# A recommendation model's embedding sums on TensorE: two units counted in a row, then their eight sums

## The chip, the cores and the metric

The kernel runs on one core of one Trainium2 chip. The metric is the device time of one execution in microseconds (us), the median of several runs. Each core has five engines with queues of their own: TensorE (PE), ScalarE (ACT), VectorE (DVE), GpSimd (POOL) and SyncE (SP, which here only starts transfers). They wait for each other by semaphores.

## What is computed

The reference is a recommendation model: a small network on 13 dense features, sums of 20 looked-up rows in each of 26 tables, all pair products of the 27 vectors of a sample, and a second network. What matters here is the sum of looked-up rows.

```
x = _mlp(dense_x, bot, sigmoid_last=False)
pooled = jax.vmap(lambda tab, ix: jnp.take(tab, ix, axis=0).sum(axis=1))(tables, indices)
Tcat = jnp.concatenate([x[:, None, :], jnp.transpose(pooled, (1, 0, 2))], axis=1)
Z = jnp.einsum('bim,bjm->bij', Tcat, Tcat)
R = jnp.concatenate([x, Z[:, li, lj]], axis=1)
return _mlp(R, top, sigmoid_last=True)
```

There are 2048 samples, 26 tables of 12500 rows by 64 numbers, and 20 indices per sample and table.

## The kernel before

Five of the 26 tables are gathered by POOL with indirect transfers (L598) and summed on DVE (L1071). The other 21 (TP in the code) are never gathered. For them the kernel builds, for each block of 512 samples, a matrix of counts (how often does sample b use row r), and multiplies the table with it on PE. A table has four blocks.

**Counting.** A block's samples lie in 86 groups of 6. Four groups make a unit, so a block has 22 units (UNITS), the last with two groups only. DVE builds one-hot factors for a pair of units at a time (`onehot_pair`, L1037 and L1042), in two buffers. PE multiplies them (`count_unit`, L659): eight matmuls of 60 rows by 99 columns for a unit, four for the last. A unit's result fills two PSUM banks: banks 0 and 1 for even units, 2 and 3 for odd ones (`unit_ps[u % 2]`). ACT copies it to SBUF as integers (`unpack_unit`, L820), whose bytes are read as fp8 counts afterwards. PE may write unit n only when the copy of unit n-2 is done (the wait at L652), and, for an even unit, when its pair of one-hots is there (L650).

**Summing.** With a block's counts complete, 98 matmuls (`sum_rows`, L678), each of 128 table rows by 512 samples, add up into one bank (`acc[k % 2]`). The table is stored as a high and a low fp16 part; ACT makes them in seven chunks, the high part at L782 and the low at L789, with a subtraction on DVE between (L998). ACT (`take_lo`, L811) and DVE (`pool_bags`, L1048) take the sum away.

**The order.** `phase(t, k, tn, kn)` is written out by hand for PE: it sums block k of table t and counts the next block between, so phase 0 counts block 1, and phase 3 counts block 0 of the next table. Each of its 22 rounds counts one unit and does PER_UNIT = 4 sums; the last 10 sums follow the last round. `await_rows` holds the waits for the counts of the whole block (L671), for a free accumulator (L672) and for the chunks of the table (L674, in phase 0 only). In phase 0, `turn_bags` (L641) stands ahead of unit 6, and behind the phase the transposes of the next table's indices (L633). A table is one turn of a loop; the last table stands behind the loop, and its phase 3 has only sums.

ACT's order is fixed too, unit by unit, with other work between the copies. In phase 3 the high part of a chunk comes after units 5, 8, 12, 15 and 19, the low part after 9, 12, 16 and 19. In phase 0 there is a high part after units 0 and 2, L811 after unit 1, low parts after 4, 6 and 8, a copy of gathered sums (L803) after 10 and the conversion of indices (L795, L797) after 12. In phases 1 and 2 only L811 stands between, after unit 1. DVE works two pairs ahead of PE; before the third pair of phase 0 it has `pool_bags` and the copy of coefficients (L1005). In phase 1 it also takes the maximum of the next table (L970).

Ahead of all this stands the first network (L624), and behind it the pair products (L745) and the second network, which the change doesn't touch.

Of the kernel before, what the change touches and what calls it, by code (L numbers as in the profile page):

```python
# [47 lines left out]
def build(nc, dense_x, indices, tables, w_bot, b_bot, w_top, b_top, out):  # L48
# [6 lines left out]
    SPAN = -(-ROWS // P)  # L55
# [16 lines left out]
    UNITS = -(-GROUPS // UG)  # L72
# [30 lines left out]
    def units_of(u):  # L103
        return range(u * UG, min((u + 1) * UG, GROUPS))

    ctx = ExitStack()
    with ctx:
# [264 lines left out]
        PER_UNIT = 4  # L372
# [244 lines left out]
        def _(pe):  # L617
# [19 lines left out]
            def turn_bags(n, done):  # L637

                pe.wait_ge(piece_free, PIECES + PIECES * done)
                for q in range(GPAIRS):  # L640
                    last = nc.tensor.transpose(bags_ps[:, q * P:(q + 1) * P],  # L641
                                               bags_out[:, 2 * q:2 * q + 2, :].rearrange("p c d -> p (c d)"),
                                               ident[:, :])
                last.then_inc(bags_turned, 1)

            def count_unit(t, k, u, first=False):

                n = UNITS * (BLOCKS * t + k) + u
                if u % 2 == 0:
                    pe.wait_ge(onehots_ready, PAIRS * (BLOCKS * t + k) + u // 2 + 1)  # L650
                if not (first and u < 2):
                    pe.wait_ge(counts_ready, n - 1)  # L652
                r = (PAIRS * k + u // 2) % 2
                for g in units_of(u):
                    x = g % UG
                    sub, lane = u % 2 * SUBS + x // LG, x % LG
                    for h in range(HALVES):
                        rows_h = slice(h * HP, h * HP + HK)
                        last = nc.tensor.matmul(unit_ps[u % 2][:, h, x * HC:(x + 1) * HC],  # L659
                                                onehot_p[rows_h, r, sub, :, lane],  # L660
                                                onehot_c[rows_h, r, sub, :, :, lane].rearrange("p c s -> p (c s)"),
                                                start=True, stop=True)
                        if g == units_of(u)[-1]:
                            last.then_inc(unit_counted, 1)

            def await_rows(t, k, j0, j1):

                n = BLOCKS * t + k
                if j0 == 0:
                    pe.wait_ge(counts_ready, UNITS * n + UNITS)  # L670
                    pe.wait_ge(acc_free, n + 1)  # L671
                for j in range(j0, j1):  # L672
                    if k == 0 and j % CJ == 0:
                        pe.wait_ge(parts_ready, CHUNKS * t + j // CJ + 1)  # L674

            def sum_rows(t, k, j):

                mm = nc.tensor.matmul(acc[k % 2][:, 0:NB], parts[:, j, :],  # L678
                                      count_bytes[k % 2][:, j % COLS, 0:NB, j // COLS],
                                      start=(j == 0), stop=(j == SPAN - 1))  # L680
                if j == SPAN - 1:
                    mm.then_inc(block_summed, 1)
                elif k == BLOCKS - 1 and j % CJ == CJ - 1:
                    mm.then_inc(chunk_used, 1)

            def phase(t, k, tn, kn, bags=False):

                for u in range(UNITS):
                    if bags and u == 6:
                        turn_bags(t, GB * t)  # L690
                    j1 = SPAN if u == UNITS - 1 else PER_UNIT * (u + 1)
                    await_rows(t, k, PER_UNIT * u, j1)
                    count_unit(tn, kn, u)
                    for j in range(PER_UNIT * u, PER_UNIT * (u + 1)):
                        sum_rows(t, k, j)
                for j in range(PER_UNIT * UNITS, SPAN):
                    sum_rows(t, k, j)
# [12 lines left out]
            with pe.Fori(0, TP - 1) as t:  # L710
                phase(t, 0, t, 1, bags=True)
                turn_indices(t + 1)
                phase(t, 1, t, 2)
                phase(t, 2, t, 3)
                phase(t, 3, t + 1, 0)
# [498 lines left out]
```

## Time and profile before

| | |
|---|---|
| median of 3 runs | 3051.23 us (3049.17 to 3052.97) |
| the profiled execution | 3058.61 us, of which span 3056.8 us |
| mean granted TensorE clock | 0.963 of full speed |
| PE busy | 2934.3 us (96%), 24204 matmuls |
| ACT busy | 2182.6 us (71%) |
| DVE busy | 1991.5 us (65%) |
| POOL busy | 1759.3 us (58%) |
| chain that ended last | PE 85%, ACT 7%, issue 5% |

The span runs from the first instruction to the last in one profiled execution. Busy time is time with an instruction at work; matmuls follow each other before the one ahead has ended, so 96% doesn't say that PE is at its peak. The chain is followed back from the last instruction through whatever released each step.

### The profile page before, as it was taken

The page shows a single profiled execution, that of the slowest core. Times are in us where ns is not written, and L with a number is a line of the kernel's source. Part 1 is how long each engine was busy: PE and PEld are TensorE (multiplying, and loading weights), DVE is VectorE, ACT ScalarE, POOL GpSimd, SP SyncE. Part 2 cuts the span into 40 slices and gives each one's busy share as a digit, 9 for nine tenths or more (in the row PEclk, how much of TensorE's full clock was granted, in tenths as well). Part 3 has the DMA queues.
Part 4 walks back from the last instruction along what each step waited for, and adds up shares of the span by engine and source line. Part 5 has one row for each costly group of instructions (what it writes and reads, how often), then busy time and mean ns, then how long its engine had stood idle before and what let it go on. Part 6 is the DMA issues. An engine that isn't in the chain of part 4 may idle for free.

```text
span 3056.8 us, 65500 instructions
## 1 busy us (share of the span) xinstructions
PE 2934.3 (96%) x24204; PEld 1249.3 (41%) x24204; DVE 1991.5 (65%) x3358; ACT 2182.6 (71%) x2496; POOL 1759.3 (58%) x1640
## 2 busy tenths in 40 slices
PE   6999999999999999999999999999999999999798
PEld 2333343333433333333333333333333333337574
DVE  4477676776767767677676776767767677643221
ACT  3678778777777777877778778777777877872232
POOL 3266676666766667676676666766667676300000
PEclk8899999999999999999999999999999999997668
DMA  2112122121221212212122121221212212007711
GB/s 66 59 29 72 28 72 70 29 72 27 73 69 29 71 28 73 69 30 71 28 73 69 30 71 27 73 69 29 71 28 73 69 30 69 17 25 119 129 35 29
DMA packets 173103, 167.99 MB, mean 55 GB/s; under 512 B 116105, under 2 KB 134329, under 8 KB 167477
## 3 DMA queue, kind: packets, MB, share of 16 engines
q1 hardware_dynamic: 121380, 110.94, 13.2%
q0 software_dynamic: 51200, 52.53, 8.7%
q8 instruction: 238, 3.90, 0.5%
q10 hardware_dynamic: 272, 0.52, 0.1%
q14 instruction: 13, 0.10, 0.0%
HBM read 143.83 MB, written 20.05 MB: 54 GB/s over the span
## 4 chain that ended last, share of the span: by engine, by line
PE 85%; ACT 7%; issue 5%; SPq 1%; DMA 1%; DVE 0%; ACTq 0%; POOL 0%; DVEq 0%; POOLq 0%
PE ps L678 59%; PE ps L659 16%; PE ps L624 5%; PE ps L745 4%; ACT counts L820 4%; ACT parts L782 2%; ACT parts L789 1%; SPq L496 0%; ACT h_bot L833 0%; ACT pooled_sb L811 0%; SPq L519 0%; DMA look_in<-in_r_indices 0%; DMA pooled<-pooled_sb 0%; DMA products<-zt 0%; SPq L503 0%
## 5 line engine op out<-in xcount | busy, mean ns | idle before, releaser
L598 POOL DMA_INDIRECT rows<-in_L_rec_tables,look x1600 | 1745.2, 1091 | 834.3 <-issue 474.2
L820 ACT CAST counts<-ps 128x792 int32<-128x792 f32 (+1 forms) x1848 | 1773.0, 979 | 583.3 <-PE ps L659 571.1
L678 PE MATMUL ps<-counts,parts 128*128 128x512 fp8e3 x8232 | 2178.4, 390 | 0.0
L1037 DVE TENSOR_TENSOR onehot_p<-iota_by_unit,place 128x1024 bf16<-128x1024 bf16 x924 | 636.6, 689 | 639.1 <-PE ps L659 613.4
L678 PEld LDWEIGHTS ps<-counts,parts 128*128 128x128 f16 x8232 | 646.8, 96 | 755.6 <-issue 6.2
L659 PEld LDWEIGHTS ps<-onehot_c,onehot_p 60*128 60x128 bf16 x14448 | 382.4, 95 | 876.1 <-issue 758.2
L659 PE MATMUL ps<-onehot_c,onehot_p 60*128 60x99 bf16 x14448 | 666.5, 209 | 55.0 <-ACT counts L820 35.2
L1042 DVE TENSOR_TENSOR onehot_c<-column_c,weighted_s 128x792 bf16<-128x792 bf16 x924 | 521.7, 565 | 0.0
L1071 DVE TENSOR_REDUCE rows<-rows 128x64 f32<-128x384 f32 (+1 forms) x240 | 188.1, 784 | 9.0 <-DVE pooled_sb L1048 9.0
L998 DVE SCALAR_TENSOR_TENSOR raw<-raw,coef_next,parts 128x896 f32<-128x896 f32 x147 | 168.4, 1146 | 18.1 <-ACT parts L782 18.1
L381 DVE COPY zt<-ps 32x208 f32<-32x208 f32 x128 | 64.8, 507 | 152.4 <-PE ps L745 150.5
L1048 DVE SCALAR_TENSOR_TENSOR pooled_sb<-ps,coef,pooled_sb 64x512 f32<-64x512 f32 x84 | 62.0, 738 | 145.8 <-ACT pooled_sb L811 145.8
L782 ACT ACTIVATE parts<-raw,coef_next 128x896 f16<-128x896 f32 x147 | 155.8, 1060 | 1.0
L970 DVE TENSOR_REDUCE rowmax<-raw 128x1 f32<-128x896 f32 x147 | 156.1, 1075 | 0.0
L1024 DVE TENSOR_TENSOR column_c<-iota_by_unit,place 128x2904 bf16<-128x2904 bf16 x84 | 140.5, 1672 | 3.9
L745 PE MATMUL ps<-slots 64*128 64x104 f32 x1024 | 138.9, 456 | 4.2 <-DMA slots<-pooled 4.2
L789 ACT ACTIVATE parts<-raw 128x896 f16<-128x896 f32 x147 | 142.0, 966 | 0.0
L745 PEld LDWEIGHTS ps<-slots 64*128 64x128 f32 x1024 | 138.2, 367 | 6.1 <-issue 6.1
L381 ACT COPY zt<-ps 32x208 f32<-32x208 f32 x128 | 63.4, 496 | 87.6 <-PE ps L745 86.1
L624 PE MATMUL ps<-feats,w_top0T 128*128 128x512 f32 (+1 forms) x128 | 68.5, 677 | 20.1 <-DMA feats<-products 15.4
L811 ACT ACTIVATE pooled_sb<-ps,coef 64x512 f32<-64x512 f32 x84 | 57.4, 683 | 26.1 <-PE ps L678 24.1
L613 POOL MEMSET slots<- 128x1280 f32 x2 | 2.3, 1165 | 120.8 <-PE ps L678 120.8
(82 smaller groups left out, 525.4 us busy)
## 6 DMA issues: line engine op xcount, KB each, us to landing
raw<-in_L_rec_tables SPq DMA_DIRECT2D x21, 1792.0 KB, 8.3
raw<-in_L_rec_tables SPq DMA_DIRECT2D x21, 1344.0 KB, 11.8
rows<-in_L_rec_tables,look POOLq DMA_INDIRECT x1600, 2.5
pooled<-pooled_sb SPq DMA_DIRECT2D x84, 128.0 KB, 2.3
slots<-pooled SPq DMA_DIRECT2D x30, 352.0 KB, 7.9
products<-zt SPq DMA_DIRECT2D x16, 351.0 KB
idx_raw<-in_r_indices SPq DMA_DIRECT2D x42, 79.7 KB
gathered<-bags_t SPq DMA_DIRECT2D x42, 64.0 KB
```

The lines of the kernel that those rows point to most:

```text
L598: nc.gpsimd.indirect_dma_start(rows[:, s, l, :], None, rows_flat, bass.IndirectOffsetOnAxis(ap=look[:, c, s * PL + l:s * PL + l + 1].bitca ...
L624: last = nc.tensor.matmul(into[i % len(into)][0:mm, :], w, x, start=(k == 0), stop=(k == len(terms) - 1))
L659: last = nc.tensor.matmul(unit_ps[u % 2][:, h, x * HC:(x + 1) * HC], onehot_p[rows_h, r, sub, :, lane], onehot_c[rows_h, r, sub, :, :, lan ...
L678: mm = nc.tensor.matmul(acc[k % 2][:, 0:NB], parts[:, j, :], count_bytes[k % 2][:, j % COLS, 0:NB, j // COLS], start=(j == 0), stop=(j == ...
L745: last = nc.tensor.matmul(banks[2 * ((b + half) % 4) + x // 4][:, x % 4 * P:x % 4 * P + GW], tiles[half][:, g, :, :].rearrange("p k s -> p ...
L782: nc.scalar.activation(parts[:, c, 0:D], raw[:, c, :], ACT.Copy, scale=coef_next[:, 2:3]).then_inc(hi_ready, 1)
L789: nc.scalar.activation(parts[:, c, D:2 * D], raw[:, c, :], ACT.Copy, scale=2.0 ** LO_SHIFT).then_inc(parts_ready, 1)
L820: nc.scalar.copy(counts[k % 2][:, :, u * UG * GS:(u * UG + g) * GS].rearrange("p c (g h s) -> p h g c s", h=HALVES, s=HS), unit_ps[u % 2][ ...
L998: nc.vector.scalar_tensor_tensor(raw[:, c, :], raw[:, c, :], coef_next[:, 2:3], parts[:, c, 0:D], ALU.mult, ALU.subtract).then_inc(diff_re ...
L1037: tt(onehot_p[:, r, :, :, :], iota, at, ALU.is_equal)
L1042: tt(onehot_c[:, r, :, :, :, :], cols, mask, ALU.mult).then_inc(onehots_ready, 1)
L1071: nc.vector.tensor_reduce(dst, src, AX.X, ALU.add).then_inc(piece_free, 1)
```

## The change

PE's phase now goes by pairs of units. It waits for the table rows of both, counts the even unit (banks 0 and 1) and the odd unit (banks 2 and 3), and then does the eight sums of both. The last pair is followed by the ten sums left over, so it has 18. Only PE's order changes; the other engines' instructions stay as they are.

```diff
             def phase(t, k, tn, kn, bags=False):
 
-                for u in range(UNITS):
+                for u in range(0, UNITS, 2):
                     if bags and u == 6:
                         turn_bags(t, GB * t)
-                    j1 = SPAN if u == UNITS - 1 else PER_UNIT * (u + 1)
+                    j1 = SPAN if u == UNITS - 2 else PER_UNIT * (u + 2)
                     await_rows(t, k, PER_UNIT * u, j1)
                     count_unit(tn, kn, u)
-                    for j in range(PER_UNIT * u, PER_UNIT * (u + 1)):
+                    count_unit(tn, kn, u + 1)
+                    for j in range(PER_UNIT * u, PER_UNIT * (u + 2)):
                         sum_rows(t, k, j)
                 for j in range(PER_UNIT * UNITS, SPAN):
                     sum_rows(t, k, j)
```

On PE, in the loop's phase 0, units 4 and 5 before (x is the number of matmuls; REGISTER_ALU rows compute the value that the next wait asks for):

```order
L650 REGISTER_ALU
L652 REGISTER_ALU
L659 MATMUL ps<-onehot_c,onehot_p 128x99 x8
L678 MATMUL ps<-counts,parts 128x512 x4
L652 REGISTER_ALU
L659 MATMUL ps<-onehot_c,onehot_p 128x99 x8
L678 MATMUL ps<-counts,parts 128x512 x4
```

and the same two units in the change:

```order
L650 REGISTER_ALU
L652 REGISTER_ALU
L659 MATMUL ps<-onehot_c,onehot_p 128x99 x8
L652 REGISTER_ALU
L659 MATMUL ps<-onehot_c,onehot_p 128x99 x8
L678 MATMUL ps<-counts,parts 128x512 x8
```

The four sums of the even unit moved behind the odd unit's counts, and the odd unit's wait now stands between two runs of counts.

On PE, the end of phase 0 before, from unit 20:

```order
L650 REGISTER_ALU
L652 REGISTER_ALU
L659 MATMUL ps<-onehot_c,onehot_p 128x99 x8
L678 MATMUL ps<-counts,parts 128x512 x4
L674 REGISTER_ALU
L652 REGISTER_ALU
L659 MATMUL ps<-onehot_c,onehot_p 128x99 x4
L678 MATMUL ps<-counts,parts 128x512 x14
L629 ISA
```

and in the change, into the start of phase 1:

```order
L674 REGISTER_ALU
L650 REGISTER_ALU
L652 REGISTER_ALU
L659 MATMUL ps<-onehot_c,onehot_p 128x99 x8
L652 REGISTER_ALU
L659 MATMUL ps<-onehot_c,onehot_p 128x99 x4
L678 MATMUL ps<-counts,parts 128x512 x18
L629 ISA
L633 MATMUL ps<-ident,idx_raw 128x86 x4
L670 REGISTER_ALU
L671 REGISTER_ALU
L650 ISA
L652 ISA
L659 MATMUL ps<-onehot_c,onehot_p 128x99 x16
L678 MATMUL ps<-counts,parts 128x512 x8
```

The last pair has 12 counts and 18 sums in a row. In a phase's first pair the wait for the whole last block covers the second unit too, so its 16 counts stand without a step between.

## Rows read from the trace of the kernel before

**Rows 1.** The page: busy times, and the chain that ended last by engine and line.
```profile
PE 2934.3 (96%) x24204; PEld 1249.3 (41%) x24204; DVE 1991.5 (65%) x3358; ACT 2182.6 (71%) x2496; POOL 1759.3 (58%) x1640
...
PE 85%; ACT 7%; issue 5%; SPq 1%; DMA 1%; DVE 0%; ACTq 0%; POOL 0%; DVEq 0%; POOLq 0%
PE ps L678 59%; PE ps L659 16%; PE ps L624 5%; PE ps L745 4%; ACT counts L820 4%; ACT parts L782 2%; ACT parts L789 1%; SPq L496 0%; ACT h_bot L833 0%; ACT pooled_sb L811 0%; SPq L519 0%; DMA look_in<-in_r_indices 0%; DMA pooled<-pooled_sb 0%; DMA products<-zt 0%; SPq L503 0%
```

**Rows 2.** Windows of a table: length, PE, PEld, DVE, ACT, POOL busy, clock, DMA.
```profile
1419.42:1450.56 31.14, 31.14 (x276) 12.63 (x276) 26.51 (x45) 22.05 (x23) 20.76 (x20) 1.00 0.15 30
1450.56:1481.41 30.85, 30.85 (x271) 12.22 (x272) 20.73 (x41) 21.99 (x23) 23.32 (x24) 1.00 0.14 29
1481.41:1546.25 64.84, 62.22 (x543) 24.68 (x544) 44.45 (x70) 55.00 (x64) 42.79 (x39) 1.00 0.26 77
```

**Rows 3.** Page, groups: line engine op, shapes xcount | busy us, mean ns | idle before.
```profile
L820 ACT CAST counts<-ps 128x792 int32<-128x792 f32 (+1 forms) x1848 | 1773.0, 979 | 583.3 <-PE ps L659 571.1
```

**Rows 4.** Order of time, PE: start us, us, engine line, [idle before]; starts of phases 1 and 2.
```profile
1545.98 0.27 PE L659 MATMUL ps<-onehot_c,onehot_p 60*128 60x99 bf16 x4
1546.18 3.33 PE L678 MATMUL ps<-counts,parts 128*128 128x512 fp8e3 x14
...
1549.74 0.36 PE L659 MATMUL ps<-onehot_c,onehot_p 60*128 60x99 bf16 x8
1550.04 1.08 PE L678 MATMUL ps<-counts,parts 128*128 128x512 fp8e3 x4
1551.05 0.37 PE L659 MATMUL ps<-onehot_c,onehot_p 60*128 60x99 bf16 x8
...
1580.58 0.37 PE L659 MATMUL ps<-onehot_c,onehot_p 60*128 60x99 bf16 x8
```

**Rows 5.** Order of time, ACT, start of phase 2 (unit 0, and L811 after unit 1).
```profile
1581.01 0.98 ACT L820 CAST counts<-ps 128x792 int32<-128x792 f32 x1 [2.99 <-PE ps L659]
...
1583.33 0.68 ACT L811 ACTIVATE pooled_sb<-ps,coef 64x512 f32<-64x512 f32 x1
```

**Rows 6.** Order of time, ACT, in phase 3.
```profile
1496.32 1.04 ACT L782 ACTIVATE parts<-raw,coef_next 128x896 f16<-128x896 f32 x1
1497.26 0.98 ACT L820 CAST counts<-ps 128x792 int32<-128x792 f32 x1
1498.13 0.94 ACT L789 ACTIVATE parts<-raw 128x896 f16<-128x896 f32 x1
1498.98 2.73 ACT L820 CAST counts<-ps 128x792 int32<-128x792 f32 x3
...
1503.34 2.81 ACT L820 CAST counts<-ps 128x792 int32<-128x792 f32 x3
```

**Rows 7.** Order of time, PE: counts behind a wait, in phase 3 and phase 0.
```profile
1504.43 0.36 PE L659 MATMUL ps<-onehot_c,onehot_p 60*128 60x99 bf16 x8 [0.22 <-ACT counts L820]
...
1516.64 0.36 PE L659 MATMUL ps<-onehot_c,onehot_p 60*128 60x99 bf16 x8 [0.79 <-issue]
...
1523.59 0.37 PE L659 MATMUL ps<-onehot_c,onehot_p 60*128 60x99 bf16 x8 [1.61 <-ACT counts L820]
```

**Rows 8.** Waits: engine line waited for, us in total, times, longest us.
```profile
POOL rows L598 <- DVE rows L1071: 359.4, 109, 52.4
```

**Rows 9.** Order of time, DVE, ahead of the third pair of phase 0.
```profile
1520.59 0.74 DVE L1048 SCALAR_TENSOR_TENSOR pooled_sb<-ps,coef,pooled_sb 64x512 f32<-64x512 f32 x1 [5.87 <-ACT pooled_sb L811]
...
1522.90 0.56 DVE L1042 TENSOR_TENSOR onehot_c<-column_c,weighted_s 128x792 bf16<-128x792 bf16 x1
```

**Rows 10.** Windows, columns as in rows 2: granted clock (0.65) in one phase 0.
```profile
759.00:763.00 4.00, 4.00 (x27) 1.55 (x26) 4.00 (x7) 2.49 (x4) 0.44 (x1) 0.65 0.10 10
```

**Rows 11.** Chain in order of time: the last 14 sums of phases 2 and 0.
```profile
715.98 3.26 PE ps L678 x14
...
782.20 3.26 PE ps L678 x14
```

**Rows 12.** Order of time, weight loads (PEld) of the last 14 sums of a phase.
```profile
1577.32 2.82 PEld L678 LDWEIGHTS ps<-counts,parts 128*128 128x128 f16 x14
```

## Prediction, made before the changed kernel had run

> **What bounds the kernel now.** The page's first line comes first [rows 1]: TensorE (PE) is busy 96% of the span, ScalarE (ACT) 71%, VectorE (DVE) 65%. In the chain of waits PE holds 85%, ACT 7%, of which L820, the copy of counted units, 4%. So time taken off PE's own sequence counts, as long as ACT keeps up. The windows by stage [rows 2] split a table of 126.8 us. Phases 1 and 2 (31.14 with the turning of indices, 30.85) have no idle PE at all. Phases 3 and 0 together take 64.84 with PE busy 62.22; 2.6 us is waiting. ACT's 1848 copies of counts, 979 ns each, are most of its work [rows 3].
>
> PE in order of time [rows 4] shows a unit: eight counts, four sums, next counts 1.31 us behind the first. What does the alternation cost? A row of 14 sums lasts 3.33 us, one of 4 1.08: 0.225 for each more sum. Eight counts last 0.36, four 0.27: 0.0225 for each more count. But the next counts begin 1.01 behind the start of four sums, which is 4 x 0.225 = 0.90 plus 0.11; and sums begin 0.30 behind the start of eight counts, which is 8 x 0.0225 = 0.18 plus 0.12. So a round of two crossings costs about 0.2, though PE reads as busy, since each matmul's record reaches past the start of the next. It isn't the wait ahead of a unit: unit 1 of a phase (start 1551.05) has none ahead of it, since the wait for the whole last block covers it, and its crossing costs the same.
>
> **The change, part by part.** It adds and removes no instruction of work. Each pair of units has one round of crossings where it had two. The rows are rounded and the first of a run comes a little slower than the others, so of 0.19 to 0.23 I take 0.195. A pair takes 2 x 1.305 - 0.195 = 2.41 us. In a phase of 11 pairs, the last one with 12 counts and 18 sums, that is 2.15 us, if nothing waits.
>
> What ACT allows has to be laid against this. From the rows: a copy starts 0.43 behind the start of its unit's counts (1580.58, 1581.01) and takes 1.0 [rows 4, 5]. Three copies in a row last 2.73, so they follow at 0.87; a high part (L782) holds ACT 0.94, a low part (L789) 0.85 [rows 6]. PE goes on close behind the end of the copy waited for: the first of three copies from 1503.34 ends 1.04 later (2.81 less two steps of 0.87 to 0.89), and the counts start at 1504.43, so I take 0.06 [rows 6, 7].
>
> Take s as the start of a pair. Copy A runs s+0.43 to 1.43, copy B s+1.30 to 2.30. The next pair's second unit writes the banks of B at s+2.41+0.20 = 2.61 and needs it at 2.36: **0.25 to spare**, where a unit now has 1.1. The next pair's first unit has 0.9 to spare. ACT itself is idle 0.67 in each pair. So phases 1 and 2 run free, also with L811 (0.68) after unit 1, and gain 2.15 each. DVE is not in the way: it was busy 26.5 of 31.1 us in phase 1 [rows 2] and its pair of one-hots is released once per pair, a unit earlier than now against its use. POOL loses slack but waits 359 us in all on DVE [rows 8], 18 per table, of which 4 go.
>
> Phase 3 has five high and four low parts between the copies. After an odd unit one costs nothing (idle 0.67 plus 0.25 absorb it). After an even unit it stands between A and B: B is ready at s+3.3 instead of 2.36, and PE waits 0.6 to 0.7. Laid out in order: high part after unit 8, wait 0.65 at unit 11; the low part after 9 leaves 0.15 at 13; high and low after 12 put B at s+4.1, wait 1.35 at 15; low after 16, 0.55 at 19. New waits 2.7; the old ones in that phase were about 0.35 (one of 0.3 stands in [rows 7]). Net: -2.15 + 2.7 - 0.35 = **0.2 to 0.3 longer**.
>
> Phase 0: its third pair waits now, at 1523.59 [rows 7]. The name given is ACT, but the copy it needs was long done. One-hots finished at 1522.90 + 0.56 [rows 9], after a chain: copy 0, high part, copy 1, L811, DVE's L1048 (from 1520.59), coefficients, one-hots. It starts 0.43 behind the phase and ACT works without a gap, so unit 4 again starts 6.95 behind unit 0, and what the first two pairs save is lost. The other nine save 9 x 0.195 = 1.75; low parts after units 4, 6, 8 and the conversion after 12 are all after even units and cost 0.35, 0.2, 0.35 and 0.4. Net gain 0.4.
>
> A table: 2.15 + 2.15 + 0.4 - 0.3 = 4.4. Twenty tables 88, the last one's three phases (0 to 2) 4.7: **-92.7**. Start and tail stay.
>
> The clock: the granted clock falls to its lower level (1.2 GHz) behind some of the waits at unit 4 of phase 0 [rows 10]; the stretch from phase 2's last sums to phase 0's then takes 66.2 us (715.98 to 782.20) instead of 64.8, 1.4 to 1.5 more [rows 11]. Six of twenty tables have this. The 1.7 us wait now becomes 0.65 and 1.3 with eight sums between; I take half of the six as gone, -4.5. Ends: all gone -9, all twenty +21.
>
> Sum -97. The profiled execution, 3058.6 in all, would be 2961; the median shown is 3051.2, 0.24% lower, so **2954**.
>
> **The inner boundary** is the one price that no row shows: counts on counts, with a register step and a wait between. Nearest row: inside a run, 0.0225 per count, no gap (my value; unit 1 of a phase with and without such a step crosses alike). Far end: as much as a crossing, 0.1, or more; next rivals. A gain from it is excluded, as PE can't start counts faster than within a run.
>
> **Rivals.**
> (B) The inner wait makes PE drain as a crossing does: 0.09 of the 0.195 stays. Phases 1 and 2 gain 1.15 each, phase 0 0.15, phase 3 loses 0.8: -1.7 per table, -34 and -2.4 for the last: **3015**. For: the second unit's wait resolves only 0.25 before its use, so it is not met far ahead. Against: in [rows 7], after real waits, eight counts still last 0.36.
> (C) No change, **3051**: there is no price for crossing; each unit's first weight load and each sum's load stands exposed whatever the order. The rows speak against it: 14 loads of sums take 2.82 within 3.33 of gapless sums [rows 4, 12]. The Trainium skill (TensorE: Matmul & The Clock Gate, Part 3 on packing small matmuls) says that a weight load overlaps running matmuls only where it uses another row group. By that rule sums could never hide their loads and longer runs would gain nothing; this case's trace disagrees for sums on sums. It may be why a crossing costs something, which the trace doesn't tell.
> (D) Slower: the wait in the middle of a pair. If PE reaches the second unit's counts late, by issue or because ACT's second copy comes 0.45 later than laid out, each pair pays more than the 0.195 it saves. PE's restart of the loop shows that issue can cost 0.79 [rows 7]. At 0.25 lost per inner boundary phases 1 and 2 grow by 0.6 each, 0 by 0.6, 3 by 1.6: +3.5 per table, **3121**. It decides from 0.2 on. Against: close copies follow at 0.87 in [rows 6] and the margin of 0.25 is on top.
>
> **Chances.** (A) the forecast 78%, (B) 12%, (C) 4%, (D) 6%. Within A: waits in phases 0 and 3 may be off by 0.5 us per table (10 us), the crossing by 0.01 (18 us over some 900 pairs, half of it eaten by waits), the clock by -5 to +10: 2935 to 2976. The range goes on to take in B: 2935 to 3018; left out are C, D and a few per cent at either side. About 0.2%, 6 us, is what a measurement of this kernel can tell from no change: faster 0.90, same 0.04, slower 0.06.
>
> **What would show it.** In phases 1 and 2: runs of 16 counts (0.55) and 8 sums (1.98), pairs at 2.41, a phase of 28.7, no idle PE. Phase 3 of 32.3 with PE waiting on L820 at units 11, 15, 19; phase 0 near 32.5 with unit 4 at 6.95. Sums at 0.225, copies at 1.0 as before. ACT's share of the chain goes up from 7% to over 9%. The forecast is wrong if a phase 1 isn't near 28.7 (B: 29.7, C: 30.85), or if waits at odd units appear in phases 1 and 2 (D).

## The result, and the profile after

The changed kernel takes 2935.3 us in the median of four runs (2932.4 to 2937.8), the kernel before 3051.0 (3049.2 to 3053.0): a ratio of 0.962 with a 95% interval of 0.9604 to 0.9637, 115.7 us less. The forecast of 2954 was 97 less; its direction and its main term were right, its range (from 2935) holds the result by 0.3 us.

The page of the changed kernel, busy times and chain (lines behind L691 have moved on by one: L821 is the copy of counts, L783 and L790 the high and low parts, L812 the part of the block sum on ACT):

```profile
PE 2770.4 (94%) x24204; PEld 1308.6 (45%) x24204; DVE 1991.6 (68%) x3358; ACT 2121.8 (72%) x2496; POOL 1830.7 (62%) x1640
...
PE 78%; ACT 14%; issue 5%; SPq 1%; DMA 1%; ACTq 1%; DVE 0%; POOL 0%; DVEq 0%; POOLq 0%
```

Against [rows 1], PE's busy time fell by 164 us with the same 24204 matmuls, and the span by 121; ACT's share of the chain doubled from 7% to 14%. Who waited for whom on PE (us in total, times, longest):

```profile
PE ps L659 <- ACT counts L821: 85.5, 153, 2.2
...
PE ps L659 <- issue: 7.9, 24, 0.6
```

Before, these were 35.2 us and 17.0 us.

The windows of the four phases of one table, first before, then after (columns as in [rows 2]; here each phase begins at its first counts):

```profile
1388.37:1422.92 34.55, 32.88 (x277) 13.39 (x278) 21.55 (x34) 26.70 (x32) 21.54 (x21) 0.95 0.38 123
1422.92:1453.75 30.83, 30.83 (x271) 12.19 (x270) 27.42 (x45) 22.05 (x23) 20.75 (x19) 1.00 0.15 30
1453.75:1484.60 30.85, 30.85 (x271) 12.22 (x271) 20.50 (x39) 21.99 (x23) 22.88 (x24) 1.00 0.14 29
1484.60:1516.64 32.04, 31.03 (x271) 12.19 (x271) 22.31 (x34) 28.40 (x32) 22.43 (x21) 1.00 0.13 26
```

```profile
1333.35:1366.00 32.65, 30.08 (x278) 13.70 (x278) 21.37 (x34) 26.00 (x32) 21.72 (x19) 1.00 0.38 129
1366.00:1394.57 28.57, 28.57 (x272) 12.91 (x272) 27.32 (x45) 20.89 (x23) 22.22 (x21) 1.00 0.16 34
1394.57:1423.11 28.54, 28.54 (x272) 12.88 (x272) 20.37 (x39) 20.93 (x23) 22.56 (x22) 1.00 0.13 29
1423.11:1454.73 31.62, 29.47 (x272) 12.98 (x272) 22.51 (x34) 28.41 (x32) 24.91 (x23) 1.00 0.12 28
```

The table of before shown here is one with a clock drop (granted clock 0.95 in its phase 0); without it phase 0 takes 33.11. Over the twenty tables of the loop the means are 33.11, 30.84, 30.85, 31.97 before and 32.66, 28.56, 28.55, 31.55 after, phase 0 without the tables that have a drop: six before, one after. So a table gained 0.45 + 2.28 + 2.30 + 0.42 = 5.4 us, twenty tables 109, the last table's three phases 5.4. The six drops of before cost 9.0 us in all. The one after is in the first table, where the granted clock of phase 0 was 0.90 and the phase took 3.1 us more (35.72):

```profile
117.40:153.13 35.73, 32.50 (x277) 14.49 (x278) 20.86 (x32) 24.20 (x30) 18.40 (x17) 0.90 0.38 125
```

Together that is 109 + 5.4 + 6.0 = 120 of the 121 us between the two spans.

PE in order of time at the start of phase 1, after; compare [rows 4]:

```profile
1482.53 0.47 PE L659 MATMUL ps<-onehot_c,onehot_p 60*128 60x99 bf16 x12
1482.93 4.23 PE L678 MATMUL ps<-counts,parts 128*128 128x512 fp8e3 x18
1487.00 0.46 PE L633 MATMUL ps<-ident,idx_raw 86*128 86x86 f32 x4
1487.39 0.56 PE L659 MATMUL ps<-onehot_c,onehot_p 60*128 60x99 bf16 x16
1487.88 1.98 PE L678 MATMUL ps<-counts,parts 128*128 128x512 fp8e3 x8
1489.79 0.56 PE L659 MATMUL ps<-onehot_c,onehot_p 60*128 60x99 bf16 x16
1490.29 1.98 PE L678 MATMUL ps<-counts,parts 128*128 128x512 fp8e3 x8
1492.19 0.56 PE L659 MATMUL ps<-onehot_c,onehot_p 60*128 60x99 bf16 x16
```

A pair takes 2.40 (1489.79 to 1492.19) where two units took 2.61. The pair at 1487.39 has no wait inside, that at 1489.79 has one; both last the same 0.56. The inner boundary costs nothing that shows.

PE in phase 3, after, from unit 10:

```profile
1435.31 0.36 PE L659 MATMUL ps<-onehot_c,onehot_p 60*128 60x99 bf16 x8
1436.01 0.37 PE L659 MATMUL ps<-onehot_c,onehot_p 60*128 60x99 bf16 x8 [0.34 <-ACT counts L821]
...
1440.82 0.36 PE L659 MATMUL ps<-onehot_c,onehot_p 60*128 60x99 bf16 x8
1442.33 0.37 PE L659 MATMUL ps<-onehot_c,onehot_p 60*128 60x99 bf16 x8 [1.14 <-ACT counts L821]
...
1446.93 0.36 PE L659 MATMUL ps<-onehot_c,onehot_p 60*128 60x99 bf16 x8
1447.74 0.36 PE L659 MATMUL ps<-onehot_c,onehot_p 60*128 60x99 bf16 x8 [0.44 <-ACT counts L821]
...
1450.33 4.23 PE L678 MATMUL ps<-counts,parts 128*128 128x512 fp8e3 x18
1454.73 0.56 PE L659 MATMUL ps<-onehot_c,onehot_p 60*128 60x99 bf16 x16 [0.17 <-issue]
```

These are the waits that were laid out, at units 11, 15 and 19: the second unit's counts start 0.70, 1.51 and 0.81 behind the first's instead of 0.20. The last line of the fence is what was not foreseen: 0.17 idle at the restart of the loop, which was 0.79 [rows 7].

### The profile page after: what moved, and what is told of

It reads as the page before. It is cut to its first block, busy times and chain, and to the rows that moved or that the text cites. A ratio compares the mean times of both kernels' runs of the same rounds, so it can differ in the third digit from the quotient of the medians.

```text
span 2935.9 us, 65496 instructions
## 1 busy us (share of the span) xinstructions
PE 2770.4 (94%) x24204; PEld 1308.6 (45%) x24204; DVE 1991.6 (68%) x3358; ACT 2121.8 (72%) x2496; POOL 1830.7 (62%) x1640
## 4 chain that ended last, share of the span: by engine, by line
PE 78%; ACT 14%; issue 5%; SPq 1%; DMA 1%; ACTq 1%; DVE 0%; POOL 0%; DVEq 0%; POOLq 0%
PE ps L678 55%; PE ps L659 13%; ACT counts L821 7%; PE ps L624 5%; PE ps L746 4%; ACT parts L783 3%; ACT parts L790 3%; ACTq L818 0%; SPq L496 0%; ACT h_bot L834 0%; ACT idx_raw L798 0%; DMA pooled<-pooled_sb 0%; SPq L519 0%; DMA look_in<-in_r_indices 0%; SPq L503 0%
## 5 line engine op out<-in xcount | busy, mean ns | idle before, releaser
L598 POOL DMA_INDIRECT rows<-in_L_rec_tables,look x1600 | 1814.2, 1134 | 652.7 <-issue 467.8
L821 ACT CAST counts<-ps 128x792 int32<-128x792 f32 (+1 forms) x1848 | 1708.2, 973 | 523.9 <-PE ps L659 506.8
L678 PE MATMUL ps<-counts,parts 128*128 128x512 fp8e3 x8232 | 2015.7, 388 | 0.0
L678 PEld LDWEIGHTS ps<-counts,parts 128*128 128x128 f16 x8232 | 717.3, 96 | 910.3 <-issue 2.4
L659 PE MATMUL ps<-onehot_c,onehot_p 60*128 60x99 bf16 x14448 | 545.2, 208 | 98.6 <-ACT counts L821 85.5
L659 PEld LDWEIGHTS ps<-onehot_c,onehot_p 60*128 60x128 bf16 x14448 | 371.5, 95 | 543.0 <-ACT counts L821 348.0
L783 ACT ACTIVATE parts<-raw,coef_next 128x896 f16<-128x896 f32 x147 | 153.4, 1044 | 1.0
L790 ACT ACTIVATE parts<-raw 128x896 f16<-128x896 f32 x147 | 138.9, 945 | 0.0
L812 ACT ACTIVATE pooled_sb<-ps,coef 64x512 f32<-64x512 f32 x84 | 57.6, 685 | 26.3 <-PE ps L678 24.2
```

Source lines behind the costliest of these rows:

```text
L598: nc.gpsimd.indirect_dma_start(rows[:, s, l, :], None, rows_flat, bass.IndirectOffsetOnAxis(ap=look[:, c, s * PL + l:s * PL + l + 1].bitca ...
L678: mm = nc.tensor.matmul(acc[k % 2][:, 0:NB], parts[:, j, :], count_bytes[k % 2][:, j % COLS, 0:NB, j // COLS], start=(j == 0), stop=(j == ...
L783: nc.scalar.activation(parts[:, c, 0:D], raw[:, c, :], ACT.Copy, scale=coef_next[:, 2:3]).then_inc(hi_ready, 1)
L790: nc.scalar.activation(parts[:, c, D:2 * D], raw[:, c, :], ACT.Copy, scale=2.0 ** LO_SHIFT).then_inc(parts_ready, 1)
L821: nc.scalar.copy(counts[k % 2][:, :, u * UG * GS:(u * UG + g) * GS].rearrange("p c (g h s) -> p h g c s", h=HALVES, s=HS), unit_ps[u % 2][ ...
```

## Experiments

Every ratio and difference is to runs of the kernel before on the same chip, whose medians were 3051 to 3053 us, unless another kernel is named. e3, e6 and e11 have one run each, so no interval is given for them.

**Where the gain is: pairs in two phases only.** Edit of the kernel before, shortened (e1; e2 has `k in (0, 3)`):

```diff
-                for u in range(UNITS):
+                step = 2 if k in (1, 2) else 1
+                for u in range(0, UNITS, step):
...
-                    count_unit(tn, kn, u)
+                    for v in range(u, u + step):
+                        count_unit(tn, kn, v)
```

> Pairs of units only in phases 1 and 2; phases 0 and 3 as before. Crossing theory (a round of two crossings costs 0.2 us and phases 1 and 2 wait for nothing): each of these phases 28.56 instead of 30.85, so -2.29 x 2 x 21 = -96 us, 2955. Phases 0 and 3 stay at 33.1 (34.6 with a clock drop) and 32.0. Rival (the gain of the change came mostly from the clock and the loop's restart): under -50.

> Pairs of units only in phases 0 and 3. Crossing theory with ACT's waits: what is left of the change's -116, about -20 us, 3031: phase 0 32.65, no clock drop (-9 in all), phase 3 31.55 with 2.75 of waits at odd units and a restart of the loop that is 0.5 shorter. Phases 1 and 2 30.85.

Measured: e1 2956.2 us, ratio 0.9685 (0.9669 to 0.9702), -97; e2 3030.4 us, ratio 0.9932 (0.9915 to 0.9949), -23. Together that is -120, and the change alone -116. One window of each, phase 1 of e1 and phase 3 of e2:

```profile
1374.88:1403.44 28.56, 28.56 (x271) 12.89 (x271) 27.42 (x45) 20.87 (x23) 20.85 (x19) 1.00 0.18 33
```

```profile
1469.84:1501.28 31.44, 29.47 (x271) 12.98 (x271) 22.46 (x34) 28.36 (x32) 23.91 (x20) 1.00 0.13 26
```

Five sixths of the gain lie in the two phases in which ACT has almost nothing but copies. e1's phase 0 is that of before (33.11), yet behind its first table it has no clock drop, where before has five. So drops can be missing with the old phase 0 as well, and that the change has none behind its first table isn't shown to be its doing.

**Is it the crossing?** The kernel before, with more crossings and no more waits (e3; the part of the edit in `phase`, the other part lets `count_unit` do half a unit):

```diff
-                    count_unit(tn, kn, u)
-                    for j in range(PER_UNIT * u, PER_UNIT * (u + 1)):
-                        sum_rows(t, k, j)
+                    for part in range(2):
+                        if u < UNITS - 1 or part == 0:
+                            count_unit(tn, kn, u, part=part)
+                        for j in range(PER_UNIT * u + 2 * part, PER_UNIT * u + 2 * part + 2):
+                            sum_rows(t, k, j)
```

> The kernel before, with each unit cut in two: 4 counts, 2 sums, 4 counts, 2 sums (the last unit stays whole). No wait is added. Crossing theory: 21 more rounds a phase at 0.2 each, phases 1 and 2 35.2 instead of 30.85; phases 0 and 3 somewhat less than that much longer since they waited; in all +340 to +370 us, about 3400. Rival (the pause belongs to a unit's waits and register steps, not to the switch between kinds of matmul): within 20 us of before, 3051.

Measured: 3416.5 us in the one run, +363. A window of its phase 1, and PE in order of time (its L661 and L680 are the counts and sums):

```profile
1599.43:1634.63 35.20, 35.20 (x271) 11.01 (x270) 27.74 (x45) 22.07 (x23) 21.53 (x21) 1.00 0.15 28
```

```profile
1530.38 0.27 PE L661 MATMUL ps<-onehot_c,onehot_p 60*128 60x99 bf16 x4
1530.58 0.62 PE L680 MATMUL ps<-counts,parts 128*128 128x512 fp8e3 x2
1531.14 0.27 PE L661 MATMUL ps<-onehot_c,onehot_p 60*128 60x99 bf16 x4
```

21 more rounds cost 35.20 - 30.83 = 4.37 us, 0.208 each; the change takes 11 away and gains 2.28, 0.207 each. PE is busy without a gap in all three. Rival (C), no price for crossing, and the rival of a pause that belongs to a unit's waits are out.

What a switch costs is thus shown, why is not. The two kinds of matmul differ in rows, columns, number type and PSUM bank at once, and no run takes these apart. The weight loads (PEld) of before give a hint. Here they stand at a switch beside the matmuls that use them:

```profile
1501.83 0.57 PEld L678 LDWEIGHTS ps<-counts,parts 128*128 128x128 f16 x4
1501.84 1.08 PE L678 MATMUL ps<-counts,parts 128*128 128x512 fp8e3 x4
...
1502.84 0.21 PEld L659 LDWEIGHTS ps<-onehot_c,onehot_p 60*128 60x128 bf16 x8 [0.44 <-issue]
1502.85 0.36 PE L659 MATMUL ps<-onehot_c,onehot_p 60*128 60x99 bf16 x8
```

Within a run of sums each load starts 0.22 us ahead of its matmul, during the one before. The load of the first matmul behind a switch starts only with it (0.004 ahead in the records), in both directions. The first counts then start 0.32 behind the last sum instead of 0.226, 0.09 more, and a load lasts 0.095. A load that isn't done ahead would fit the price; that it is the cause is not tested.

**Does the inner wait matter?** The change, with both waits for ACT ahead of the even unit's counts (e4; the edit in `count_unit`, which both calls now get with `waited=True`):

```diff
-                if not (first and u < 2):
-                    pe.wait_ge(counts_ready, n - 1)
+                if not (first and u < 2) and not (waited and u % 2):
+                    pe.wait_ge(counts_ready, n if waited else n - 1)
```

> The change, with the odd unit's wait for ACT moved ahead of the even unit's counts, so that 16 counts stand without a wait between. If the inner wait costs nothing by itself: phases 1 and 2 stay at 28.56 as long as copy B (ready 2.36 behind the pair's start) is there before 2.40; phases 0 and 3 wait as long or up to 0.2 longer per waiting pair (8 of them: up to +1.6 per table, +32 us). So 2935 to 2967. If the inner wait drains PE: phases 1 and 2 get shorter by up to 11 x 0.05 = 0.5.

Measured: 3012.1 us, ratio 0.9872 (0.9855 to 0.9888): 77 more than the change, where at most 32 was expected. Phases 1 and 2 stayed near (28.73, with 0.17 once, behind ACT's L812), phase 0 went to 34.36 and phase 3 to 33.15 on average. PE in its phase 0, and ACT beside it:

```profile
1504.86 0.56 PE L659 MATMUL ps<-onehot_c,onehot_p 60*128 60x99 bf16 x16 [0.74 <-ACT counts L821]
1505.36 1.98 PE L678 MATMUL ps<-counts,parts 128*128 128x512 fp8e3 x8
1508.07 0.56 PE L659 MATMUL ps<-onehot_c,onehot_p 60*128 60x99 bf16 x16 [0.74 <-ACT counts L821]
```

```profile
1505.29 1.01 ACT L821 CAST counts<-ps 128x792 int32<-128x792 f32 x1 [0.49 <-PE ps L659]
```

Where PE waits for both copies, ACT mostly has nothing left to do until the next counts are done: it idles 0.49 at eight of the ten places of a table where PE waits over 0.2, and the pair shown takes 3.21 (1504.86 to 1508.07). With the wait inside the pair, the even unit is counted while ACT still copies the odd one, and ACT goes on without a pause. So the inner wait is free by itself and worth 77 us where it stands.

**The restart of the loop.** Three arrangements of phase 3's end (edits shortened). e5: the kernel before with only its last two units in a row. e6: the kernel before with 8 sums behind unit 20 and 10 behind unit 21. e11: the change with its last two units apart.

```diff
 # e5
+                starts = list(range(UNITS)) if k < BLOCKS - 1 else list(range(UNITS - 1))
+                for u in starts:
+                    step = 2 if k == BLOCKS - 1 and u == UNITS - 2 else 1
 # e6
+                    if k == BLOCKS - 1 and u == UNITS - 2:
+                        j1 += PER_UNIT
+                    elif k == BLOCKS - 1 and u == UNITS - 1:
+                        j0 += PER_UNIT
+                        j1 += PER_UNIT
 # e11
+                    step = 1 if k == BLOCKS - 1 and u >= UNITS - 2 else 2
```

> The kernel before, with only the last two units of phase 3 counted in a row, so that 18 sums instead of 14 stand ahead of the loop's branch. Theory (the branch and the first fetch of the next turn take a fixed time that only the sums still queued cover): the idle time before phase 0, 0.89 on average now, falls by up to 4 x 0.225 = 0.9, by about 0.5 as in the change; with one round of crossings 0.2 less, phase 3 takes 31.3 instead of 32.0, -14 us in all (3037 to 3040), less if clock drops come or go (1.5 each). Rival (the restart shrank because of pairs elsewhere in the phase): -4 us, phase 3 at 31.8.

> The kernel before, with four of the last 14 sums of phase 3 moved ahead of the last unit's counts, so that 10 stand ahead of the branch. Same matmuls, same number of crossings. Theory of the covered branch: 4 x 0.225 = 0.9 more idle before phase 0 in each of 20 tables, phase 3 at 32.9, +18 us. Rival: no change, 32.0.

> The change with the last two units of phase 3 apart again, so that 14 sums instead of 18 stand ahead of the loop's branch; everything else in pairs. If the restart is covered by the last 14 to 17 matmuls that the trace shows started after the branch (2.9 to 3.4 us of work, most when all are sums), the idle time before phase 0 goes back from 0.25 to 0.8 or so and one crossing comes back: phase 3 31.55 + 0.55 + 0.2 = 32.3, +15 us, 2951. Rival (the shorter restart comes from pairs elsewhere): +4 us, phase 3 at 31.75.

Measured: e5 3040.2 us, ratio 0.9954 (0.9939 to 0.9969), phase 3 31.38. e6 3050.3, phase 3 31.79: no slower. e11 2954.0, 19 more than the change where 15 was expected, phase 3 32.4. The counts behind the restart, in one table each of e5 and e6:

```profile
748.65 0.36 PE L659 MATMUL ps<-onehot_c,onehot_p 60*128 60x99 bf16 x8 [0.36 <-issue]
```

```profile
750.54 0.27 PE L659 MATMUL ps<-onehot_c,onehot_p 60*128 60x99 bf16 x4
750.75 2.43 PE L678 MATMUL ps<-counts,parts 128*128 128x512 fp8e3 x10
753.95 0.37 PE L659 MATMUL ps<-onehot_c,onehot_p 60*128 60x99 bf16 x8 [0.78 <-issue]
```

Taking 14 sums to 18 shortens the restart, taking 18 back to 14 undoes it. From the last sum's start to phase 0's first counts it takes, on average over the 19 restarts, 1.17 us in before, 0.50 in the change, 0.47 in e5 and 1.18 in e11; where the loop ends instead, it takes 0.32. But with 10 sums in e6 it takes 0.97. So it isn't the length of the last run, as e6 expected.

The records of PE's sequencer show the loop's branch, which is 3.3 to 3.9 us long when it goes back and 0.08 when it doesn't. When it begins, 14 matmuls are still to start in before and e11, and 17 in the change, e5 and e6 (in e6 three sums, four counts and ten sums). The next counts come 3.9 to 4.5 behind its beginning, 4.2 on average in before, the change, e5 and e11 and 4.1 in e6. What hides the restart is how long the matmuls that are left take: the last of them starts 3.02 behind the branch in before and e11, 3.12 in e6 and 3.72 in the change and e5. So e6's shorter run is made up for by the branch, which comes three matmuls earlier. That reading was made after e6 and has e11 for it. The 4.2 isn't fixed, however: e2, with the same 18 sums as the change, has 4.07, and no idle time at any restart. What sets it, and how early the branch comes, stays open.

**Giving ACT's other work a better place.** e7 is the change with every high and low part, the bag copy and the index conversion moved behind odd units (the main part of the edit; it also makes one high part fewer in the start and leaves out its wait for a used chunk):

```diff
-            hi_after = {-(-CJ * (q + 1) // PER_UNIT) + 1: q for q in range(CHUNKS - 2)}
-            lo_after = {u + 4: q for u, q in hi_after.items() if u + 4 < UNITS}
+            hi_after = {5: 0, 7: 1, 11: 2, 15: 3, 19: 4}
+            lo_after = {9: 0, 13: 1, 17: 2, 21: 3}
...
-                    if u == AHEAD:
-                        make_hi(t, CHUNKS - 1)
-                    elif u in (4, 6, 8):
-                        make_lo(t, CHUNKS - 3 + (u - 4) // 2)
-                    elif u == 10:
+                    if u in (3, 5):
+                        make_hi(t, CHUNKS - 2 + (u - 3) // 2)
+                    elif u in (7, 9, 11):
+                        make_lo(t, CHUNKS - 3 + (u - 7) // 2)
+                    elif u == 13:
                         copy_bags(t)
-                    elif u == 12 and t is not TP - 1:
+                    elif u == 15 and t is not TP - 1:
...
                 unpack_unit(t + 1, 1, 0)
-                make_hi(t + 1, CHUNKS - 2)
```

e8 adds this on DVE (and the third pair of the first table's block 1 in the start), e10 is the change with this alone, e9 is the kernel before with both moves:

```diff
                 for d in range(AHEAD, PAIRS):
-                    onehot_pair(t, 1, d)
+                    if d > AHEAD:
+                        onehot_pair(t, 1, d)
...
+                onehot_pair(t + 1, 1, AHEAD)
                 pool_bags(t, 3)
```

> The change, with ACT's high and low parts, bag copy and index conversion each moved behind an odd unit, one at a time: in phase 3 high parts after 5, 7, 11, 15, 19 and low parts after 9, 13, 17, 21; in phase 0 high parts after 3 and 5 (none between copies 0 and 1), low parts after 7, 9, 11, bags after 13, indices after 15. Theory (a part between the two copies of a pair costs PE 0.6, behind both about 0.1 to 0.2): phase 3 falls by 1.5 to 30.0, phase 0 by 2.0 to 30.6, in all -3.5 x 20 = -70 us against the change, about 2865. Rival (ACT's total load is the bound, the place doesn't matter): within 10 us of the change, 2935.

> As e7, and DVE makes the one-hots of the third pair of block 1 ahead of its last part of the block sum (L1048) and the coefficients. Theory (the wait at unit 4 of phase 0 is for these one-hots): the wait of 1.0 at unit 4 left in e7 goes, phase 0 falls by 0.7 to 29.9; about -14 us against e7, 2851. Rival (that wait is for ACT's copy, as the trace names it): as e7.

> The kernel before (units one by one), with the same moves on ACT and DVE as e8. Theory (ACT's place matters little where a lone copy has 1.1 to spare, much where a pair's second has 0.25): only the wait at unit 4 of phase 0 (1.5) and 0.35 in phase 3 go, phase 0 31.4, phase 3 31.7, about -1.9 x 20 = -38 us, 3014; phases 1 and 2 at 30.85. Rival (the moves are worth the same with and without pairs, -65 as from the change to e8): 2987.

> The change with the move on DVE alone (one-hots of the third pair ahead of L1048), ACT as in the change. Theory: the wait of 1.5 at unit 4 of phase 0 goes, since it is for one-hots, but the copy of unit 3, which stands behind L812 and a high part, is late instead: about 1.0 at unit 5. Phase 0 32.1 instead of 32.65, -10 us against the change, 2925. Rival (the wait at unit 4 is for ACT, as the trace names it): phase 0 stays at 32.65, wait at unit 4 as before.

| | median us | ratio to before (95%) | phases 0 to 3, mean (0 without a clock drop) |
|---|---|---|---|
| change | 2935.3 | 0.962 (0.9604 to 0.9637) | 32.66, 28.56, 28.55, 31.55 |
| e7 | 2875.8 | 0.9418 (0.9405 to 0.9431) | 30.80, 28.56, 28.55, 30.34 |
| e8 | 2870.1 | 0.9401 (0.9388 to 0.9413) | 30.47, 28.56, 28.55, 30.33 |
| e9 | 3011.8 | 0.9871 (0.9854 to 0.9887) | 31.53, 30.84, 30.85, 31.59 |
| e10 | 2929.0 | 0.9601 (0.9585 to 0.9617) | 32.31, 28.57, 28.55, 31.53 |

PE in phase 3 of e7, from unit 12, and ACT beside it:

```profile
1405.98 0.75 PE L659 MATMUL ps<-onehot_c,onehot_p 60*128 60x99 bf16 x16
1406.67 1.98 PE L678 MATMUL ps<-counts,parts 128*128 128x512 fp8e3 x8
1408.58 0.83 PE L659 MATMUL ps<-onehot_c,onehot_p 60*128 60x99 bf16 x16
```

```profile
1406.17 1.07 ACT L783 ACTIVATE parts<-raw,coef_next 128x896 f16<-128x896 f32 x1
1407.10 1.89 ACT L821 CAST counts<-ps 128x792 int32<-128x792 f32 x2
1408.83 1.00 ACT L790 ACTIVATE parts<-raw 128x896 f16<-128x896 f32 x1
```

The two copies of a pair now stand together, and a pair with a part behind it loses 0.2 to 0.3 (16 counts last 0.75 to 0.83 instead of 0.56) where one part between the copies cost 0.5 to 0.6 and two 1.3. e7 gained 59 us on the change, against 70 expected: phase 3 has seven waits of 0.17 to 0.29, 1.6 together, where 0.1 to 0.2 each was expected. For its phase 0 the trace of e7 names another cause of the wait at unit 4 than that of before did:

```profile
PE ps L659 <- DVE onehot_c L1042: 16.8, 21, 1.4
```

e8 makes it go, but gains only 6 us of the 14 expected, as ACT's copies are then late at units 9 and 11 (0.25 and 0.19). In e10 the waits moved as expected, from unit 4 to unit 5, where one of 1.03 stands on average:

```profile
1332.83 0.36 PE L659 MATMUL ps<-onehot_c,onehot_p 60*128 60x99 bf16 x8
1334.09 0.36 PE L659 MATMUL ps<-onehot_c,onehot_p 60*128 60x99 bf16 x8 [0.89 <-ACT counts L821]
```

Its gain on the change was 6 us and not 10, and the intervals of the two ratios overlap; that phase 0 is 0.35 shorter comes from the traces. e9 gained 40 us without pairs, about the 38 expected; with pairs the same moves gain 65. So the pairs make the place of ACT's work matter more, though not alone. e8 is the fastest version, 183 us below before.

## Why the prediction was right, and where it was off

- **The crossing**, "of 0.19 to 0.23 I take 0.195": 0.208 by the change and by e3. Phases 1 and 2 gained 2.29 each instead of 2.15, 6 us over 42 phases. They never wait, as laid out.
- **The inner boundary**, my value of no gap: right. Rival (B) is out, 28.56 and not 29.7. Rival (D) is out as well: no pair of phases 1 and 2 waits, so the margin of 0.25 was enough in all of them.
- **ACT's waits in phase 3**, 2.7 us: 2.6 at units 11, 13, 15 and 19 as laid out, and 0.18 at unit 9. **Phase 0**: gain 0.45 instead of 0.4; new waits of 0.37, 0.22, 0.38 and 0.42 behind ACT's work after units 4, 6, 8 and 12 (0.35, 0.2, 0.35 and 0.4 were laid out), and unit 4 again about 6.95 behind unit 0. That this wait is for one-hots, although the trace names ACT, was shown by e10, which moves only them and has no wait there.
- **The line that was off** is "Start and tail stay" with phase 3's "0.2 to 0.3 longer": the restart of the loop was carried over as it was, at 1.17 us from the last sum to the next counts, and it fell to 0.50, since 18 sums stand ahead of it. That is 0.67 us at each of 19 restarts, 13 us; with the larger crossing phase 3 became 0.42 shorter instead of 0.3 longer, 14 us in all. With the 6 us of phases 1 and 2 this is the difference between -97 and -116. The long last run was named in the forecast ("12 counts and 18 sums") and the restart's idle time was in [rows 7]; they weren't put together.
- **The clock**, half of six drops gone, -4.5: five are gone and the one left, in the first table, cost twice as much as each of the six, -6.0 in the two profiles. The count came out near, but not for a reason that is shown: e1, with the old phase 0, also has a drop in its first table alone. The medians can't tell 4 us apart from it.
- **The range** held by 0.3 us, with two of the four runs below 2935. The mechanism and the direction were right by the rows; that the median still fell inside was luck, as the range had no term for the restart.

## What to carry to other kernels

A switch between two kinds of matmul cost PE about 0.1 us each way here without any idle time showing: compare the spacing within long and short runs. When work is batched to save switches, lay the consumer's queue against the new order: here ACT had 1.1 us to spare per unit before, and 0.25 for the second of a pair after, so whatever stands between two copies came back as a wait of PE until it was moved behind both. Take each buffer's wait as late as it can stand: waiting for both at once cost 77 us. And ask what the new order puts ahead of a loop's branch.

## What was not expected of the hardware

A restart of the loop took PE 3.9 to 4.5 us from its branch to the next matmul, most of it hidden by the 14 or 17 matmuls that were still to start: 0.78 us of idle time was left on average in before and 0.12 in the change.

The granted clock fell in the phase 0 of some tables and not of others like them. Behind the first table it did so in five tables of the profile of before, five of e3, two each of e5 and e6 and none of the nine others, e1 with the same phase 0 among them. In the first table it fell in before, the change, e1, e6, e7, e8 and e9, and not in the other six. The waits ahead of it don't tell the tables apart: in the first table of the change PE had waited 1.40 and then 2.15 us before the clock fell to its lower level (1.2 GHz), and in that of e2, which kept the full clock, 1.43 and 2.12 at the same places. What decides it stays open.
